# The retention stage reordered: VectorE spreads the keys, and each batch's transposes are issued earlier

## The reference

```python
xn = channel_group_norm(x, norm_g, norm_b, H)      # H = 16 heads of 8 channels
q = l2_normalize(xn @ qw.T)                        # norm over all 128 channels
k = l2_normalize(xn @ kw.T)
v = xn @ vw.T
dmask = jnp.where(causal[None], gammas[:, None, None] ** exponent[None], 0.0)
sim = jnp.einsum('bhnd,bhmd->bhnm', qh, kh) * scale
yh = jnp.einsum('bhnm,bhmd->bhnd', sim * dmask[None], vh)
y = y @ ow.T + ob
x = residual + y
```

## Time and profile before

| | |
|---|---|
| median of three runs | 935.7 us (933.71 to 937.73) |
| the profiled execution | 933.87 us, its span 932.0 us |
| PE busy | 855.6 us, 92% of the span |
| DVE, ACT, POOL busy | 67%, 60%, 68% |
| granted PE clock | 0.993 of full speed |

### The profile page before, as it was taken

One profiled execution on the slowest core, in us unless ns is written; L12 is line 12 of the kernel. 1 busy time (PEld: TensorE's weight loads), 2 busy tenths in 40 slices (PEclk: granted clock), 3 DMA queues, 4 the chain that ended last, 5 costly groups with the idle time before them and its releaser, 6 DMA issues.

```text
span 932.0 us, 26419 instructions
## 1 busy us (share of the span) xinstructions
PE 855.6 (92%) x10918; PEld 582.6 (63%) x10918; DVE 627.8 (67%) x1087; ACT 558.7 (60%) x1109; POOL 631.7 (68%) x503
## 2 busy tenths in 40 slices
PE   1788989999899899898998989999999999999998
PEld 1446666666667666666576665757575757575756
DVE  4884756757666667576576775858686858585854
ACT  1365656756657577566565646575766666666663
POOL 4686776886876758667777565767666676767641
PEclk9899999999999999999999999999999999999999
DMA  9311201201112011021121121213121213131101
GB/s 299 67 36 23 52 12 34 49 17 40 29 22 53 14 37 42 17 47 23 21 55 20 30 47 26 52 30 72 32 73 32 72 27 77 27 74 28 52 1 35
DMA packets 127811, 41.82 MB, mean 45 GB/s; under 512 B 103715, under 2 KB 126925, under 8 KB 127565
## 3 DMA queue, kind: packets, MB, share of 16 engines
q1 hardware_dynamic: 122516, 38.82, 18.5%
q10 hardware_dynamic: 5177, 1.31, 0.8%
HBM read 9.70 MB, written 2.10 MB: 13 GB/s over the span
## 4 chain that ended last, share of the span: by engine, by line
PE 63%; DVE 15%; POOL 10%; ACT 6%; issue 4%; DMA 1%; SPq 0%; DVEq 0%; POOLq 0%; ACTq 0%
PE pQK L1357 9%; PE pT L1269 5%; PE pT L1226 5%; PE pS L1285 5%; PE pS L1258 5%; PE pV L1324 5%; DVE m L846 4%; PE pM L1439 4%; PE pM L1303 4%; POOL rn L454 3%; PE pQK L1659 3%; PE pT L1417 3%; DVE ss L859 2%; POOL m L467 2%; PE pS L1245 2%
## 5 line engine op out<-in xcount | busy, mean ns | idle before, releaser
L454 POOL TENSOR_TENSOR rn<-rn,half_neg 128x16 f32<-128x16 f32 x64 | 187.4, 2929 | 5.3
L467 POOL TENSOR_TENSOR m<-m 128x1024 f32<-128x1024 f32 x64 | 150.9, 2358 | 0.1
L452 POOL TENSOR_SCALAR rn<-ss 128x16 f32<-128x16 f32 x64 | 16.3, 254 | 170.2 <-DVE ss L859 168.8
L1357 PE MATMUL pQK<-wqkv,hT 128*128 128x512 f32 x256 | 123.2, 604 | 5.3 <-DVE m L846 5.3
L474 POOL TENSOR_TENSOR qkn<-m,rn 128x1024 f32<-128x1024 f32 x64 | 121.7, 1902 | 5.0
L896 DVE TENSOR_REDUCE mx<-pS 128x8 f32<-128x1024 f32 x64 | 77.9, 1218 | 57.5 <-PE pS L1258 57.4
L677 ACT ACTIVATE prT<-pT 128x1024 f32<-128x1024 f32 x64 | 65.5, 1024 | 68.7 <-PE pT L1269 68.4
L640 ACT ACTIVATE sq<-pQK 128x1024 f32<-128x1024 f32 x64 | 65.4, 1022 | 35.1 <-PE pQK L1357 34.9
L859 DVE TENSOR_REDUCE ss<-sq 128x16 f32<-128x1024 f32 x64 | 77.5, 1211 | 5.2 <-ACT sq L640 5.2
L671 ACT ACTIVATE kT<-pT 128x512 f32<-128x512 f32 x64 | 38.2, 597 | 70.9 <-PE pT L1226 70.9
L898 DVE TENSOR_TENSOR pr<-pS,mx 128x1024 f32<-128x1024 f32 x64 | 78.4, 1224 | 2.2
(11 more groups left out here) (224 smaller groups left out, 1865.4 us busy)
## 6 DMA issues: line engine op xcount, KB each, us to landing
vmix<-vown SPq DMA_DIRECT2D x124, 128.0 KB, 2.7
kT<-kT SPq DMA_DIRECT2D x60, 128.0 KB, 2.7
x<-in_L_attn_x SPq DMA_DIRECT2D x4, 512.0 KB, 9.1
hT<-xnT SPq DMA_DIRECT2D x64, 32.0 KB, 1.9
xs<-in_L_attn_x SPq DMA_DIRECT2D x8, 256.0 KB, 3.2
hT<-x2T SPq DMA_DIRECT2D x64, 32.0 KB, 1.8
out<-aqkT SPq DMA_DIRECT2D x7, 256.0 KB, 2.2
wqkv<-in_L_ffn_wqkv SPq DMA_DIRECT2D x2, 768.0 KB, 9.7
```

The lines of the kernel that those rows point to most:

```text
L454: eng.tensor_tensor(rn[:, k % 2, :], rn[:, k % 2, :], half_neg[:, 0:2 * H], ALU.pow).then_inc(S["rn_done"], 1)
L467: eng.tensor_tensor(m1[:, k % 2, :], m1[:, k % 2, :], m2[:, :], ALU.add).then_inc(S["add_done"], 1)
L1357: mm = eng.matmul(pQK[:, g * 512:(g + 1) * 512], hT[:, k, :], wqkv[:, l, g * 512:(g + 1) * 512], start=True, stop=True)
```

## The change

`kx` is now made by DVE instead of POOL, straight from the transposes in PSUM (`dve_place_keys`), so ACT copies only the queries. The transposes of batch 0 go to pT instead of pM and into slot 3, ahead of the attention's values. In slot 3 and in the stage all four engines get new orders: POOL makes the norms of batch 0 ahead of `pool_scale` of slot 2; DVE does the cosine product ahead of the residual, and the sum of squares of slot 3 near the end of the stage; ACT's squares, values and query copies are calls of their own and are interleaved anew; the exponential of batch 1 goes toward the end; PE does the LayerNorm's transposes behind the last scores. In slot 0, DVE does the addition of the retention's output ahead of applying the LayerNorm. Every row of arithmetic stays.

```diff
+        def turned_bank(b):
+            return pM if b else pT
...
@@ def pool_slot
+            if k == 2 and new and new[0] == 0:
+                pool_norm(eng, count(new, k), k)
+                pool_add(eng, count(new, k), k)
+                return
             if retain:
                 pool_retention_norm(eng, new[1], 0)
+                pool_scale(eng, count(new, 2), 2)
                 return
@@ def pool_retention
+            pool_place_queries(eng, t, 0)
             pool_retention_norm(eng, t, 1)
-            for b in range(NB):
-                pool_mask_qk(eng, t, b)
-                if b + 2 < NB:
-                    pool_retention_norm(eng, t, b + 2)
+            pool_retention_norm(eng, t, 2)
+            pool_place_queries(eng, t, 1)
+            pool_retention_norm(eng, t, 3)
+            pool_place_queries(eng, t, 2)
+            pool_place_queries(eng, t, 3)
@@ def pool_mask_qk -> pool_place_queries
             eng.wait_ge(A["t_ev"], n + 1)
-            need(eng, A["st_mm"], n - 1)
-            eng.tensor_tensor(kx[:, b % 2, :, :, :],
...
+            if b == 0:
+                eng.wait_ge(LS["o_mm"], count((0, t), 0) + 1)
@@ def act_retention
+            act_retention_queries(eng, t, 0)
+            act_retention_values(eng, t, 1)
+            act_retention_squares(eng, t, 2)
+            act_place_values(eng, t, 0)
+            act_retention_values(eng, t, 2)
+            act_retention_queries(eng, t, 1)
+            act_place_values(eng, t, 1)
+            act_retention_squares(eng, t, 3)
+            act_retention_values(eng, t, 3)
+            act_retention_queries(eng, t, 2)
+            act_place_values(eng, t, 2)
+            act_retention_queries(eng, t, 3)
+            act_exp(eng, 1, count((0, t), 1))
+            act_place_values(eng, t, 3)
@@ def dve_rotate (slot 3 of layer 0)
                 dve_retention_qk(eng, t, 0)
+                eng.wait_ge(S["sq_done"], n + 1)
+                turn_cos()
                 if normed:
                     dve_residual(eng, normed, k)
-                eng.wait_ge(S["sq_done"], n + 1)
-                turn_cos()
+                dve_place_keys(eng, t, 0)
+                turn_sin()
                 if weighted:
                     dve_output(eng, weighted[2])
                 dve_retention_qk(eng, t, 1)
-                turn_sin()
-                sum_squares()
                 return
@@ def dve_slot
+            if retained:
+                dve_retention_out(eng, old[1])
             if ff and k == 0 and not is_scaled_early(ff):
                 dve_ln_apply(eng, ff)
-            if old and k == 0 and old[0] == 0:
-                dve_retention_out(eng, old[1])
+            if retained:
+                dve_retention_stats(eng, old[1])
@@ new
+        def dve_place_keys(eng, t, b):
+            n = 4 * t + b
+            shape = [P, NBL, NG, BL]
+            eng.wait_ge(A["t_ev"], n + 1)
+            need(eng, A["st_mm"], n - 1)
+            eng.tensor_tensor(kx[:, b % 2, :, :, :],
+                              turned_bank(b)[:, P:2 * P].rearrange("p (c n) -> p c n", c=NBL).unsqueeze(2).broadcast_to(shape),
+                              place_mask.unsqueeze(1).unsqueeze(3).broadcast_to(shape), ALU.mult).then_inc(A["kx"], 1)
@@ def dve_retention
+            dve_block_sums(eng, t, 0)
             eng.wait_ge(LS["qkn_done"], 4 * t + 3)
...
+            dve_block_scores(eng, t, 0)
+            dve_place_keys(eng, t, 1)
+            dve_retention_qk(eng, t, 2)
+            dve_block_sums(eng, t, 1)
+            dve_place_keys(eng, t, 2)
+            dve_block_scores(eng, t, 1)
+            dve_retention_qk(eng, t, 3)
+            dve_block_sums(eng, t, 2)
+            dve_place_keys(eng, t, 3)
+            dve_block_scores(eng, t, 2)
+            dve_block_sums(eng, t, 3)
+            dve_sum_squares(eng, count((0, t), NB - 1), NB - 1)
+            dve_block_scores(eng, t, 3)
+            if old:
+                dve_ln(eng, old)
@@ def pe_slot (slot 3 of layer 0, behind pe_wo)
+            if k == NB - 1 and new and new[0] == 0:
+                pe_retention_turn(eng, new[1], 0)
             if weighted and not (k == 0 and ff):
                 pe_values(eng, weighted[1], weighted[2], turned)
@@ def pe_retention: see the rows of PE below
```

More of the change, by code:

```diff
@@ L630, in act_slot @@
             if k == NB - 1 and new and new[0] == 0:
-                act_retention_project(eng, new[1], 0)
+                act_retention_squares(eng, new[1], 0)
+                act_retention_values(eng, new[1], 0)
             if k == 0 and turned:
@@ L653, in act_slot @@
             if k == NB - 1 and new and new[0] == 0:
-                act_retention_project(eng, new[1], 1)
+                act_retention_squares(eng, new[1], 1)
             else:
@@ L735, in act_retention_project, with act_retention_values, act_retention_queries @@
                 need(eng, A["sqq"], 2 * n + g)
-                eng.activation(asq[:, :], bank[:, g * P:(g + 1) * P], ACT.Square,
+                eng.activation(asq[:, :], qkv_banks[b % 2][:, g * P:(g + 1) * P], ACT.Square,
                                accum_out=ass[:, b % 2, g:g + 1]).then_inc(A["sqq"], 1)
-            need(eng, A["kv_mm"], n - 1)
+        def act_retention_values(eng, t, b):
+            need(eng, A["kv_mm"], 4 * t + b - 1)
             for c_ in range(NBL):
                 rows = slice(0, (c_ + 1) * BL)
-                copied = eng.activation(avm[rows, b % 2, c_, :], bank[rows, 2 * P:3 * P], ACT.Copy)
+                copied = eng.activation(avm[rows, b % 2, c_, :], qkv_banks[b % 2][rows, 2 * P:3 * P], ACT.Copy)
             copied.then_inc(A["v"], 1)
+        def act_retention_queries(eng, t, b):
+            n = 4 * t + b
+            eng.wait_ge(A["t_mm"], n + 1)
+            need(eng, A["qx"], n - 1)
+            eng.activation(aqkT[:, b % 2, 0, :], turned_bank(b)[:, 0:P], ACT.Copy).then_inc(A["t_ev"], 1)
         def act_place_values(eng, t, b):
@@ L889, in dve_rotate, with dve_sum_squares @@
             turn_sin()
+        def dve_sum_squares(eng, n, k):
+            need(eng, LS["max_ss"], n - 1)
+            eng.tensor_reduce(ss[:, k % 2, :], sq[:, :].rearrange("p (h d) -> p h d", d=DH), AX.X,
+                              ALU.add).then_inc(LS["ss_done"], 1)
         def dve_scores(eng, b, n):
@@ L1579, in pe_retention_project, with pe_retention_turn @@
                        stop=True).then_inc(A["qkv_mm"], 1)
+        def pe_retention_turn(eng, t, b):
+            n = 4 * t + b
+            eng.wait_ge(A["qk"], 2 * n + 2)
+            need(eng, A["kx"], n)
+            for g in range(2):
+                mm = eng.transpose(turned_bank(b)[:, g * P:(g + 1) * P], aqk[:, b % 2, g, :], ident)
+            mm.then_inc(A["t_mm"], 1)
         def pe_retention(eng, t, old):
[L1583 removed]
             if old:
                 eng.wait_ge(LS["xr_done"], count(old, NB - 1) + 1)
[L1586 to L1605 removed]
@@ new lines, in pe_retention @@
+            pe_retention_project(eng, t, 2)
+            eng.wait_ge(A["kx"], 4 * t + 1)
+            pe_block_values(eng, t, 0)
+            pe_block_scores(eng, t, 0)
+            pe_block_sums(eng, t, 0)
+            pe_retention_turn(eng, t, 1)
+            pe_block_values(eng, t, 1)
+            pe_retention_project(eng, t, 3)
+            pe_block_sums(eng, t, 1)
+            pe_block_output(eng, t, 0)
+            pe_retention_turn(eng, t, 2)
+            pe_block_scores(eng, t, 1)
+            pe_block_values(eng, t, 2)
@@ L1607, in pe_block_values @@
+            pe_block_sums(eng, t, 2)
+            pe_block_output(eng, t, 1)
+            pe_retention_turn(eng, t, 3)
+            pe_block_scores(eng, t, 2)
+            pe_block_values(eng, t, 3)
+            pe_block_sums(eng, t, 3)
+            pe_block_output(eng, t, 2)
+            pe_block_scores(eng, t, 3)
+            if old:
+                eng.wait_ge(A["kx"], 4 * t + 4)
+                pe_ln(eng, old)
+            pe_block_output(eng, t, 3)
         def pe_block_values(eng, t, b):
```

55 lines of the change are left out of this document (11 added, 44 removed).

## The result

| | before | with the change |
|---|---|---|
| median | 934.83 us (933.71 to 937.73) | 920.9 us (919.0 to 924.09) |
| ratio, 95% interval | | 0.9851 (0.9822 to 0.988) |
| profiled execution, its span | 933.87, 932.0 us | 919.0, 917.2 us |
| PE, DVE, ACT, POOL busy | 92, 67, 60, 68% | 94, 71, 61, 65% |
| granted PE clock | 0.993 | 0.992 |

The change makes the kernel 1.5% faster; the forecast was 920.5 us. (The median before is 934.83 with its fourth run, and was 935.7 when the prediction was made.) The page of the kernel after: busy time and share of each engine, and the chain that ended last by engine.

A forecast was written before the change was run, and what follows sets the result against it. PE, busy in 92% of the span, was taken as the bound, so only its waits could go; 2.6 us in the first step plus 1.85 in seven others made 15.6, from 935.7 to 920.1, stated as 920.5; range 911 to 933.

The forecast's parts named there:

- The start: Retention stage's start: norms ahead of `pool_scale`, batch 0's transposes ahead of values; DVE's wait falls from 3.2 to about 1.5 us.
- The spread: DVE's new `dve_place_keys`: 0.69 us each, bounds 0.684 and 1.040, priced by the score mask's row.
- The handoffs: Between batches inside the stage: PE waits of 0.8, 0.2, 0.7 and 0.2 us remain; the stage ends 2.6 us earlier.
- the bound of 3.0: PE's waits in each retention stage, about 3.0 us, taken as the most that filling the stage's gaps can give.
- The give-back: Slot 0 of the next step: the later LayerNorm delays ACT's exponential, giving back 0.75 us in each of seven steps.
- The first step: No LayerNorm in its stage and no FFN in slot 0 behind, so it gains the full 2.6 us.
- Half the gain: Rival: tighter handoffs between batches cost PE 0.8 a step, 1.0 us a step left, 928 us; chance 0.2.
- Slower: Rival: stage ends where it did, exponential still delayed 0.75 in seven steps, 941 us; chance 0.17 with its neighbours.
- More: Rival: the stage's waits of 0.7 and 0.8 vanish, exponential hidden by the copies, up to 24 us, 912; chance 0.13.
- No effect: Rival: the stage's scores still wait for POOL's queries, time unchanged; only a small part of "same", no separate chance.

The follow-up runs named there:

- the doubled spread: The changed kernel with each spread of keys done twice on DVE, the second behind the first: 932.75 us, ratio 0.9966.
- the late statistics: The changed kernel with the retention output's statistics in slot 0 behind the maximum and subtraction instead of ahead: 917.94 us, ratio 0.9821.
- the early squares: The changed kernel with DVE's sum of squares of slot 3 back ahead of the stage's block sums: 918.91 us, ratio 0.9822.

## Why the prediction was right

*The start.* Norms first and transposes ahead of the values: right. DVE's wait fell to 1.60 (said: about 1.5), the scores of batch 0 came at 244.27 (244.45), the third transposes at 248.38 (248.3). Undone singly, these two steps cost 1.32 and 1.07 us a step.

*The spread.* Two rows of the groups by form, over the whole span:

```profile
L1030 DVE TENSOR_TENSOR hidden<-pM,cst 128x512 f32<-128x512 f32 x24 | 16.6, 692 | 16.4 <-ACT aqkT L760 16.0
L1030 DVE TENSOR_TENSOR hidden<-pT,cst 128x512 f32<-128x512 f32 x8 | 5.4, 681 | 0.0
```

0.69 was said and 0.692 and 0.681 measured: reading 128x128 of PSUM four times over costs what the score mask costs, which reads 128x512 of it once. The Trainium skill's rule (GPSIMD Engine Reference, When to use GPSIMD) of about twice would have given an estimated 0.52; here the ratio is 1.040 / 0.69 = 1.5. The measurement decides, and the row was the better source.

*The handoffs.* The predicted waits of PE were 0.8, 0.2, 0.7 and 0.2, together 1.9 us, counted from start to start: what lies between two starts beyond the first one's own cost. By that count the scores of batch 0 came 240.27 - 239.58 - 0.27 = 0.4 late (the profile's idle time is 0.23). Gaps of about 0.1 behind the groups that follow made up the rest, so that the second transposes stood at 241.71 + 4.00 = 245.71 (said: 245.9) and the third at 248.38 (248.3). For the mask of batch 1 I had 0.7 and 0.2 behind it; the mask ended at 246.65 and PE began at 246.79, some 0.25 late, and the fourth transposes came at 251.22 (251.8). Behind them I had nothing, and there came two stalls of about 0.4 us each inside runs of small matmuls, which no engine's data explains (see the last section); the end came at 257.34 (257.15). So the stage's 2.5 us are close to the 2.6 partly by luck: 0.6 too much for the mask, 0.8 missing for the stalls.

Two slips stand in this part of the prediction. 259.84 - 257.15 is 2.7, not 2.6. And 2.6 saved with 1.9 left make 4.5 us of waits before, more than the bound of 3.0, "all of the waits": the 3.0 is the idle time of the windows, which is shorter than the gaps from start to start. So neither 3.0 a stage nor 24 us in all was an upper bound.

*The give-back.* Right in its mechanism, too large in size: 0.45 us, not 0.75. Moving the statistics behind the scores removed the wait, and 0.37 of the period with it. In the fourth step 2.05 were gained in all, 2.26 in the mean of the periods, where 1.85 was said. The periods differ in part by stalls of PE: the one that saved 3.2 has one of 0.68 us in slot 0 of the kernel before.

*The first step.* Here the prediction's term of 2.6 failed: it measured -0.3. From its projection in slot 3 to the copy it took 22.1 us before (59.04 to 81.13) and 20.2 now (61.15 to 81.36), 1.9 saved, and it begins 2.1 us later, so nothing is left: the first copy is at 81.4 instead of 81.1. That delay lies ahead of the reordered retention: 0.88 us when the second transposes of the attention in the first step start (54.66, now 55.54), and 1.2 more by a slower clock right behind them (last section). The sum came out near (14.8 us of span, 15.6 said) by luck, because the seven periods gave 15.8 and not the 13.7 that this cut has in the prediction (6 x 1.85, and 2.6 for the one period behind the first step, whose slot 0 has no FFN), less a tail of 0.7.

*The rivals.* "Half the gain" would have had a period some 1.0 us shorter; it is 2.26. It rested on longer waits in every handoff between batches; the fourth stage has gaps of about 0.1 there, and the doubled spread shows how they would grow: 70% of what DVE got in addition there came out on PE. "Slower" needed the stage to save under 0.75; it saves 2.5. "More" was right in that the 0.7 and 0.8 shrank, to 0.25 and 0.4, but the exponential was not hidden, and 1.0 us a stage of idle PE is left. "No effect" needed late queries: with DVE's spread no score of the fourth stage waits for POOL; with the keys back on POOL one waits 0.6.

POOL's busy time fell by 631.7 - 599.6 = 32.1 us (said: 33), DVE's rose by 19.5 (said: 22; the spreads themselves are 16.6 + 5.4 = 22.0). The stage from first projection to copy was said to last 14.6 us; it is 14.72 in the fourth and 14.9 in the mean of five.

## What to carry to other kernels

Where PE idles between stages that hand work round four engines, follow the chain to the instruction that stands ahead of a short, late-needed one on another engine (here 1.90 us ahead of 1.0 us of norms) and swap them; alone it gave 0.7% of the 1.5% here. Before adding an instruction to the path by its full duration, look how far behind it its engine next waits: 1.21 us put in front of a wait of 1.17 us cost 0.1 a step, 2.8 us spread over four places of the stage cost 2.0. Once the waits for data are gone, look at what is left inside the runs of small matmuls. An operation moved to another engine is priced best by the row on that engine with the nearest operands.

## What the runs showed of the hardware

**Stalls inside runs of small matmuls.** PE lost up to 1.09 us between two matmuls of 128x32 with nothing in the profile that it waited for. Rows of the kernel with the change:

```profile
78.66 0.25 PE L1709 MATMUL pS<-m,vx 128*32 128x32 f32 x3 [0.84 <-issue]
...
132.68 0.26 PE L1709 MATMUL pS<-m,vx 128*32 128x32 f32 x6 [1.09 <-issue]
...
252.96 0.45 PE L1709 MATMUL pS<-m,vx 128*32 128x32 f32 x28 [0.17 <-issue]
```

The waits of PE over the whole span, with the change:

```profile
PE pS L1709 <- issue: 4.3, 8, 1.1
```

and in the kernel before:

```profile
PE pS L1646 <- issue: 2.2, 3, 0.9
```

With the data waits gone, these are the largest part of what PE still loses in these matmuls, 4.3 us where 2.2 were.

They go with the loading of PE's instructions. The page shows a DMA queue of the kind instruction, in both kernels with the same line (packets, MB, share):

```profile
q8 instruction: 88, 1.44, 0.7%
```

That is 16 KB a packet, and PE's 2 x 10918 matmuls and weight loads make 248 to a packet, or 124 matmuls. In the twelve profiles here, every gap of more than 0.3 us between two short matmuls of one line in layer 0 ends 2.2 to 3.0 us after such a packet starts. The gaps stand at fixed places of PE's stream, whatever the order of the work: the one behind the 1478th matmul (at 132.68 above) is in all twelve, the one behind the 607th (78.66) in eleven, and two of them behind successive packets are 125 to 127 matmuls apart. In the stages the packets come about every 4 us (126.34, 130.42, 134.18 with the change). The kernels with the late statistics and with the early squares have a stall of 0.73 and 0.69 us in the values (the `pT<-aT,xa` matmuls), and it is at the place of the 0.18 at 249.11 with the change. So PE most likely runs out of loaded instructions where small matmuls follow each other fastest. That is argued from the coincidence; no run changed the number of instructions or their place.

**The clock behind one long wait.** In the first step PE waits, before its second transposes of the attention, for POOL's scaled q and k, which end 0.1 us ahead of them. With the change that wait was 3.45 us, and the stretch behind it ran at a granted clock of 0.53, near the lower of the two levels (1.2 GHz); eight transposes took 1.94 us:

```profile
55.54 1.94 PE L1274 MATMUL pT<-cst,qkn 128*128 128x128 f32 x8 [3.45 <-issue]
```

```profile
55.50:59.00 3.50, 3.46 (x10) 2.10 (x10) 2.24 (x4) 1.71 (x4) 3.42 (x3) 0.53 0.00 0
```

Before, the wait was 2.37 us, the clock stayed at 1.00, and the same transposes took 1.07:

```profile
54.66 1.07 PE L1226 MATMUL pT<-cst,qkn 128*128 128x128 f32 x8 [2.37 <-issue]
```

```profile
54.60:58.00 3.40, 3.03 (x46) 2.15 (x46) 3.24 (x5) 2.69 (x7) 3.22 (x3) 1.00 0.00 0
```

With the change the transposes started 0.88 us later, and from there to the first projection of the retention PE took 61.15 - 55.54 = 5.6 us instead of 59.04 - 54.66 = 4.4, together the 2.1 us by which the first stage was late.

The twelve profiles are of two kinds. In three (the kernel before, the early squares, the doubled spread) PE did the step's first transposes at the lower level, in 1.94 us, so it was busy longer; it then waited 2.37, 1.97 and 1.97 us and kept its clock. In the other nine the first transposes took 1.07 us, the wait was 3.45, and the second ones took 1.5 to 1.9. The orders of the change do not decide it: the kernel before with POOL's norms alone is among the nine, the doubled spread among the three. POOL's first norms start at 38.60 us with the change and at 37.55 before, ahead of slot 2 of the first step, where the change begins. Why the beginnings differ stays open.
